# Second experts of a two-layer transformer: gathers spread behind the scatters, first output transposes moved, more unread products

## The reference

```python
scores = softmax(xf @ gate_w.T)
vals, idx = top_k(scores.T, k)            # k = 512 tokens per expert
y = xf[idx]                               # gathered rows
y = (y - mu) * rsqrt(var + eps) * ln_w + ln_b
h = gelu(y @ fc1s[e].T + b1s[e])          # 128 -> 512
out = (h @ fc2s[e].T + b2s[e]) * kept_w   # 512 -> 128
xf = xf.at[idx].add(out)                  # experts may share tokens
x = layernorm(x + xf)
```

## Time and profile before

| what | value |
| --- | --- |
| median of three runs | 717.15 us |
| the profiled execution | 715.15 us |
| its span, first to last instruction | 713.3 us |
| mean granted TensorE clock | 0.884 |
| busy PE, DVE, ACT, GpSimd over the span | 534.2, 421.0, 333.4, 392.2 us |
| indirect gathers of this stage (L1682) | 32, 31.2 us busy, 976 ns each |
| indirect scatters (L1690) | 32, 50.8 us busy, 1589 ns each |
| chain that ended last, share of the span in L1690 | 5% |

### The profile page before, as it was taken

One profiled execution on the slowest core, in us unless ns is written; L12 is line 12 of the kernel. 1 busy time (PEld: TensorE's weight loads), 2 busy tenths in 40 slices (PEclk: granted clock), 3 DMA queues, 4 the chain that ended last, 5 costly groups with the idle time before them and its releaser, 6 DMA issues. The chain is left out here.

```text
span 713.3 us, 15913 instructions
## 1 busy us (share of the span) xinstructions
PE 534.2 (75%) x5514; PEld 360.0 (50%) x5516; DVE 421.0 (59%) x1089; ACT 333.4 (47%) x710; POOL 392.2 (55%) x634
## 2 busy tenths in 40 slices
PE   3789999999998759999279999999400258877500
PEld 2345655555554559999256777676300134433200
DVE  3868887887874355565256888787378821111006
ACT  1167677676677405555235666564400014442206
POOL 5855566565555334442535777673290045878644
PEclk9999999999999969999679999999855568998855
DMA  4554555564611012222211222211263011333347
GB/s 122 157 164 122 141 128 132 163 173 124 171 40 47 17 29 67 67 69 53 79 30 31 56 60 63 57 46 32 60 236 8 1 33 35 41 47 38 27 61 199
DMA packets 75251, 57.55 MB, mean 81 GB/s; under 512 B 14880, under 2 KB 65856, under 8 KB 75184
## 3 DMA queue, kind: packets, MB, share of 16 engines
q1 hardware_dynamic: 67008, 47.26, 24.7%
q0 software_dynamic: 7904, 9.00, 7.7%
q10 hardware_dynamic: 272, 0.41, 0.2%
HBM read 36.90 MB, written 19.48 MB: 79 GB/s over the span
## 5 line engine op out<-in xcount | busy, mean ns | idle before, releaser
L659 DVE TENSOR_REDUCE a_mx<-a_psR 128x6 f32<-128x768 f32 x128 | 121.3, 953 | 31.0 <-PE a_psR L363 29.3
L568 ACT ACTIVATE a_pr<-a_psR 128x768 f32<-128x768 f32 x128 | 103.6, 810 | 56.8 <-PE a_psR L376 55.9
L286 POOL TENSOR_SCALAR_AFFINE_SELECT a_pr<-a_pr 128x512 f32<-128x512 f32 x128 | 80.3, 636 | 79.3 <-ACT a_pr L568 79.0
L1690 POOL DMA_INDIRECT acc<-e_ot,ids x32 | 50.8, 1589 | 21.3 <-issue 8.2
L764 POOL DMA_INDIRECT e_xt<-x1d,source x39 | 37.1, 952 | 43.9 <-PE e_psX L777 32.2
L1682 POOL DMA_INDIRECT e_xg<-tab,ids x32 | 31.2, 976 | 50.3 <-POOLq L1381 40.9
L355 PE MATMUL a_psR<-a_maskA,identb 128*128 128x256 bf16 x256 | 50.8, 281 | 2.2 <-DMA a_stack<-qkd 2.1
L1016 POOL DMA_INDIRECT a_yg<-ys,slot x32 | 35.7, 1115 | 22.4 <-POOLq L714 15.0
L1719 DVE TENSOR_TENSOR e_ot<-e_psZ,e_xg 128x512 f32<-128x512 f32 x8 | 5.5, 691 | 69.8 <-PE e_psZ L1814 47.5
L383 PE MATMUL a_psO<-a_pr,a_va 128*32 128x256 f32 x512 | 40.9, 391 | 4.6 <-ACT a_onT L560 2.8
L785 PE MATMUL e_psH<-e_xT,e_w 128*128 128x128 f32 x312 | 43.4, 284 | 0.0
(11 more groups left out here) (313 smaller groups left out, 1374.4 us busy)
## 6 DMA issues: line engine op xcount, KB each, us to landing
a_stack<-qkd SPq DMA_DIRECT2D x93, 128.0 KB, 3.5
qkd<-a_hml SPq DMA_DIRECT2D x16, 384.0 KB, 2.8
fcs<-in_fc SPq DMA_DIRECT2D x16, 256.0 KB, 4.0
ys<-e_yt SPq DMA_DIRECT2D x39, 64.0 KB, 1.5
a_xall<-in_x SPq DMA_DIRECT2D x4, 512.0 KB, 4.5
x1d<-a_x SPq DMA_DIRECT2D x16, 128.0 KB, 2.0
pjs<-in_pj SPq DMA_DIRECT2D x8, 256.0 KB, 4.0
a_x1t<-x1d SPq DMA_DIRECT2D x16, 128.0 KB
```

Source lines behind the costliest of these rows:

```text
L286: g.affine_select(out=diagonal, in_=diagonal, pattern=[[0, 4], [1, 128]], compare_op=ALU.is_ge, fill=0.0, base=0, channel_multiplier=-1).t ...
L568: a.activation(pr[s][:, :, 0:3, :].rearrange("p x k q -> p x (k q)"), psR[:, r:r + 2, 0:384], ACT.Exp).then_inc(probs, 1)
L659: v.tensor_reduce(mx[b % 2][:, :, 2 * u:2 * u + 35:17], psR[:, r:r + 2, 0:384].rearrange("p x (k c) -> p x k c", c=128), AX.X, ALU.max).th ...
L1690: pool.indirect_dma_start(acc, bass.IndirectOffsetOnAxis(ap=ids[:, C * e + a:C * e + a + 1], axis=0), ot[e % 2][:, a, :], None, compute_op ...
```

## The change

The prologue gathers experts 0, 1 and 2 and half of expert 3 (14 indirect DMAs instead of the 16 that stood ahead of the first scatter). Each scatter then stands ahead of the gathers of its step: behind scatter e come the second half of expert e + 3 and the first half of expert e + 4. For expert 7 the split is one and three: one gather behind scatter 3, three behind scatter 4. PE gets 28 unread products instead of 9 at the start of the stage and 8 more between transpose_in(0) and up(0). The output transposes of expert 0 move ahead of up(1); those of the others keep their place. Nothing else is changed.

```diff
--- before.py
+++ after.py
@@ -1620,6 +1620,7 @@
 
 
 
+
     ctx = ExitStack()
     R = D + E8 + 1
     C = CAP // 128
@@ -1675,10 +1676,10 @@
 
         @block.gpsimd
         def _(pool):
-            def gather(e):
+            def gather(e, tiles=range(C)):
                 if e >= RING:
                     pool.wait_ge(o_sb, e - RING + 1)
-                for a in range(C):
+                for a in tiles:
                     pool.indirect_dma_start(xg[e % RING][:, a, :], None, tab, bass.IndirectOffsetOnAxis(
                         ap=ids[:, C * e + a:C * e + a + 1], axis=0)).then_inc(x_in[e % RING], 16)
 
@@ -1690,12 +1691,16 @@
                     pool.indirect_dma_start(acc, bass.IndirectOffsetOnAxis(ap=ids[:, C * e + a:C * e + a + 1], axis=0),
                                             ot[e % 2][:, a, :], None, compute_op=ALU.add).then_inc(added, 16)
 
+            FIRST, REST = range(C // 2), range(C // 2, C)
             for e in range(AHEAD):
                 gather(e)
+            gather(AHEAD, FIRST)
             for e in range(E8):
+                scatter(e)
                 if e + AHEAD < E8:
-                    gather(e + AHEAD)
-                scatter(e)
+                    gather(e + AHEAD, REST if e + AHEAD < E8 - 1 else range(1, C))
+                if e + AHEAD + 1 < E8:
+                    gather(e + AHEAD + 1, FIRST if e + AHEAD + 1 < E8 - 1 else range(1))
             for g in range(NG):
                 pool.wait_ge(ve_sb, g + 1)
                 nc.gpsimd.tensor_tensor(rs[:, g, :], ve[:, g, :], A["mhalf"][:, 0:G, 0], ALU.pow).then_inc(rs_sb, 1)
@@ -1815,18 +1820,25 @@
                                                A["ident"][:])
                 last.then_inc(z_ps, 1)
 
-            for _ in range(9):
-                mm(psZ[1][:, 0:128], A["ident"][:], A["ones"][:], start=True, stop=True)
+            def unread(n):
+                for _ in range(n):
+                    mm(psZ[1][:, 0:128], A["ident"][:], A["ones"][:], start=True, stop=True)
+
+            unread(28)
             pe.wait_ge(w_in, 32 * E8)
             transpose_in(0)
+            unread(8)
             up(0)
             for e in range(E8):
                 if e + 1 < E8:
                     transpose_in(e + 1)
                 down(e)
+                if e == 0:
+                    transpose_out(e)
                 if e + 1 < E8:
                     up(e + 1)
-                transpose_out(e)
+                if e >= 1:
+                    transpose_out(e)
 
 
 def build(nc, x, xT, qkv0, wo0, wo0c, router, fc, pj, qkv1, b1col, b1row, off, lin2, lin2b, gate, lnw, lnb, fc1, b1s, fc2, b2s, out):
```

## The result

The changed kernel took 725.0 us (median of 4 runs, 723.5 to 727.3) against 717.26 us beside it: a ratio of 1.0125, 95% interval 1.0098 to 1.0153. The forecast was 715.3 us, a ratio of 0.997. It was outside the range and on the other side. Later the same kernel, unchanged, had 0.9979 [0.9958, 1.0000]. The experiments show what differed between the two measurements, though not why it differed.

What follows compares the result with a forecast made beforehand. The prediction took the second experts' entry (first gather, expert 0's products, dT), then GpSimd's scatter chain, as the bound. Start -5.3 and late gathers +3.5 gave -1.8 us: 715.3 us against the 717.15 median, range 711.9 to 719.4.

Steps and rivals of the forecast that it cites:

- Part 2: Start of the stage: output transposes of expert 0 ahead of up(1) let scatter 0 begin at 597.1, 5.3 us earlier.
- Part 1: Start of the stage: unread products keep PE at full clock, so up(0) ends at 590.8 instead of 593.0.
- Rival 1: The late dT(0) stays, start gains only 2.2 us, 3.5 lost behind it: +1.3, 718.4 us; chance 0.24.
- the 28 "delay nothing": Stage start: 28 unread products take 7.0 us, to 583.6, before the first transposes can start at 584.5.
- The term of the 8 products: Between transpose_in(0) and up(0): 8 unread products hold PE until 587.18, costing 1.1 us for a busy array.
- Part 3: GpSimd's steps: those with three gathers take 11.38 us; scatter 0 to scatter 5 takes 61.7 against 61.3, +0.4.
- Part 4: Expert 7's last gathers land 12.7 us behind scatter 4's start, so output 6 makes scatter 6 1.5 to 3.2 late.
- The forecast's ends: Scatter 6's start behind scatter 4's: 22.4 us at full clock, 24.1 where PE had sat idle; upper end taken.
- S0-m: Time from scatter 0 to DVE's first moments; the forecast's loss behind scatter 0 was 3.5 us.
- Rivals 2 and 3: Late gathers don't count, GpSimd alone sets the end, 712.3 us (0.15); gathers land 3 us or more later, slower (0.10).
- One sign named for rival 3: Outputs releasing scatters 4 and 5 would show gathers behind scatters landing later than before.
- The sum: Start -5.3 us and scatter 0 to scatter 6 +3.5 give -1.8 us for the whole kernel.

Runs made afterwards that it cites:

- e1: The whole change but with 9 unread products at the start and none between the first transposes and up(0); 0.9998 to the kernel before.
- e2: The kernel before with 28 unread products at the start and 8 between transpose_in(0) and up(0), nothing else; 1.0166.
- e3: The kernel before with only the gathers split behind the scatters; 1.0008.
- e4: The kernel before with only the output transposes of expert 0 moved ahead of up(1); 1.0008.
- f2: The whole change, unchanged, measured again with signals on time; 0.9979 to the kernel before.
- f3: The whole change without the 8 unread products behind the first transposes, the 28 kept; 0.9967 to the kernel before.
- f1: The kernel before, unchanged, run again for a second trace; 1.0010 against its own kernel.
- groups 2, 4 and 5: Three later sets of follow-up kernels, each set on one chip beside the kernel before, all with signals on time; ratios 0.9942 to 1.0116.
- group 3: One set on one chip, signals on time: kernel before again, whole change again, and two variants of its unread products; ratios 0.9959 to 1.0010.
- groups 0 and 1: The first measurement of the whole change (1.0125), and the set that tried its parts one by one (0.9998 to 1.0166); both with late signals.
- e5: The whole change without the 8 unread products behind the first transposes, run in an earlier set than f3; 0.9962 to the kernel before.
- e7: The whole change with 7 and 2 unread products of 512 columns instead of 28 and 8 of 128; 0.9982 to the kernel before.
- g1: The kernel before with output transposes of expert 0 ahead of up(1) and 7 unread products of 512 columns instead of 9; 0.9942, repeated 0.9960.

## Why the prediction was wrong

**The step that failed is Part 2, with Part 1.** I took dT(0)'s 3.1 us for a constant of that place: either it stays or it goes. It was the tail of a hold on PE's signals that reaches further forward when unread products stand ahead: with 28 + 8 of them yT came 4.3 us late and the first Gelu about 6. The start was to be 5.3 us shorter and was 3.5 longer. e1 and e2, in one group with late signals, show that the unread products do it (1.0166 alone, 0.9998 without them); e3 and e4 that neither of the other parts does. Where signals are on time the same products do no such harm (f2), so the loss needs both the products and the late signals, and why the signals are late is open. Rival 1 held that the late dT stays at its price of 3.1 us, and the sentence that the 28 "delay nothing" looked only at PE's free time. No rival had the signals of PE itself.

**Part 1, the clock.** Right: up(0) took 3.70 us, with the clock at 1.00. The term of the 8 products was mis-sized: they were to cost 1.1 us and cost 0.7 (f2 against f3), and were needed for nothing. The Trainium skill, "TensorE: Matmul & The Clock Gate", section on PE-mode transpose, says that full clock doesn't engage for transposes. The traces don't agree: four took 0.63 us at full clock, 1.10 at half.

**Part 2, where signals are on time.** dT(0) to scatter 0 took 2.41 again (593.38 to 595.78 in f2: 2.40). The start came from 23.9 to 19.6, -4.3, where the forecast had -5.3. Its end point was nearly right (scatter 0 at 19.9 behind the first gather); its base, 25.2, was 1.3 later than f1's. About 0.6 of that is the late dT, which the prediction had put at 0.5, and 0.7 an up(0) that took 6.47 us there and 5.79 in f1.

**Part 3, GpSimd's steps.** Right for the steps with three gathers: 11.43 and 11.51, and 11.41 in f2, against 11.38. The three steps ahead of them were taken over from before at 38.9 us together and took 38.1, in f2 too, 0.8 less; no run here says why.

**Part 4, late gathers.** Right in kind: expert 7's normalization started 12.74 us behind scatter 4 in f2 (658.01 - 645.27, forecast 12.7), scatter 6 was released by output 6. Its size goes with the length of down(6), and so with the clock: S4 + 22.45 in the first measurement, where down(6) took 3.60 us at full clock (S4 + 22.5 in e3, also with 3.60); S4 + 23.8 to 24.2 in groups 2, 4 and 5 and in e1, where it took 4.5 to 5.3; S4 + 25.4 in group 3, where it took 6.1. The forecast's ends were 22.4 and 24.1, with 5.29 us for such a product at the upper one. S0-m grew by 3.9 in group 3 (92.6 to 96.5; forecast 3.5). That this comes so near is in part luck, as the 0.8 us less of Part 3 stand against 1.3 us more at scatter 6. Rivals 2 and 3 are out: late gathers count, and they landed on time. One sign named for rival 3, an output that releases scatter 5, did appear in the first measurement, but it cost 0.1 us and no gather was late.

**The sum** of -1.8 us agrees with group 3, where signals were on time: -0.21% of 708.6 is -1.5 us. The agreement isn't sharp, as the interval reaches from -3.0 us to 0, and the two terms read from the traces of f2 and f1 give -4.3 + 3.9 = -0.4. In the first measurement it is 3.5 at the start, 1.1 behind it, and 4.4 ahead of the stage. Of these 4.4 I can only say that the code there is the same, that the first gather stood between 569.9 and 576.2 us in the fourteen traces with signals on time, and at 578.6 to 579.6 in e2, e3 and e4, whose code there is the same too (585.0 in e1's long execution); the changed kernel's share in it isn't shown. The medians of both kernels differ by 7.7.

**What stays open.** Why PE's signals were late in groups 0 and 1, the first two in time, and in no other. The recording of the profile isn't excluded: the six traces with late signals hold about 9.6 thousand semaphore updates, the fourteen others about 10.7 thousand. Open too are the part of GpSimd's gathers in it (argued from times, tested by no run); whether there it is the number of PE's passes, their dense issue or the 8 behind the transposes that moves the hold forward (e5 and e7 never met the condition); and whether g1 keeps its gain there.

## What to carry to other kernels

An unnamed releaser in a profile is a cost without a law: before building on the place, look for every other spot where it appears and for what runs on the other engines at that time. Here all of ACT's in the trace of before fell beside GpSimd's indirect DMAs. The name alone proves nothing, though: an unnamed wait of DVE of 0.8 us (L1577) stands in traces of both kinds. Unread products that keep the clock up should reach to the first real product and no further, and a gain from them has to be measured more than once. And gathers that are issued "just in time" behind a serial chain save nothing if that chain has slack at the start and none at the end: the reserve of 15 us had paid for the last two steps.

## What the runs showed of the hardware

- In groups 0 and 1 PE's completion signals reached ACT up to 5.8 us behind the modelled end of a product in the changed kernel and up to 8.6 in e2 (the first up product ends at 593.6, the Gelus begin at 602.28), beside a series of GpSimd's indirect gathers; the last of them came 2.6 to 3.1 us behind the end of a long series, 0.2 to 0.5 us behind a pair. With signals on time ACT starts within 0.05 us of the modelled end (f1: 592.12 and 592.16). The kernel before took 717.3 us under the one condition and 708.0 to 708.8 under the other.
- In a timeline this looks like four Gelus in one piece (2.42 us) where their inputs end 0.86 us apart.
- The same unread products of 128 columns took 6.49 us at full clock (56 passes, 0.116 each), and 8.12 where the clock stood at 0.50 to 0.51 from 576 to 579 us, soon after they began at 575.59 (f2). So what they cost isn't the same in each execution.
